# A fused transformer layer: a new start for the first batch (x ahead of five weights, rope from PSUM, smaller pieces, 20 maxima ahead of the first key-major product)

## The chip, the cores and the metric

One core of one Trainium2 chip. The metric is device time in microseconds (us) of one launch; the median of three runs before is 2280.6 us (2273.85 to 2281.94). The profile is one execution of the same program.

## The reference

The input x has 32 batches of 512 tokens by 256 channels, all in float32. Per batch:

```
x = x + attn(layernorm(x))      # q, k: x @ W.T with rope on pairs of channels, 16 heads of 16
                                # softmax(q k.T / 4) @ v, then @ Wu.T + bu
x = x + ffn(layernorm(x))       # xr, xk: token mixes of x and x shifted by one token
                                # sigmoid(xr @ Wr.T) * (relu(xk @ Wk.T)**2 @ Wv.T)
```

## The kernel before, in words

The work of every engine is written out by hand, in steps. Step b runs from -3 to 33, and each works on several batches at once: the attention of batch b, the projections of batch b+1 (v) and b+2 (q, k), the statistics of batch b+3 and the feed-forward part of batch b-1. Products in float32 are made of three products of high and low parts (`hi*hi`, `lo*hi`, `hi*lo`), so one q or k tile of 128 channels by 512 tokens has six matmuls in a PSUM bank, and a v tile has twelve of half the columns.

A step has 16 units (`UNITS`; a unit is one group of four heads by one quarter of the keys), and a unit has four places `j`. At each place TensorE makes one key-major product (`score_T`, line 893: keys in rows, scaled by the exponential on ScalarE, line 653) and one query-major product (`score`, line 911). VectorE takes the row maximum of the latter (line 694), 64 per batch. These maxima run ahead of the key-major products by `LEAD = 7` units: in step -1, units 9 to 15 make scores and maxima 0 to 27 of batch 0, and step 0 goes on with 28 to 63 and with the next batch's. The place of a maximum is given by `row_max_at`. When 16 maxima of a group of four heads are there, TensorE turns them (`row_max_T`, line 941, in unit 13 of the step ahead for group 0, and in units 1, 5 and 9 for groups 1 to 3, `MAX_T`), VectorE splits them into a high and a low part (`split_max`, lines 704 and 707), and four DMAs on SP's queue put them as two more rows under q (`move_max`, line 329). The key-major product of the group waits for these (`mrow_in`), so that the exponential comes out with the maximum subtracted. After the places, the unit's `values` (line 925) sums the probabilities of the unit before times v.

Next to the second place of every unit, TensorE has some dense work (`DENSE`): v in units 1 and 2, the turn of x in unit 3 (line 949), q in 6 and 7, k in 9 and 10, products of the batches b-1 in the others. All of it shares the two banks of `d_ps`; `bank_reader` says which reader must be done before a bank is written again. The second k product uses the bank of the first one.

ScalarE copies q and k out of PSUM into `rope_t` (line 577), which has room for one tensor; GpSimd (POOL) makes the rope in six operations (lines 411 to 429) in `rot`, ScalarE makes the high part (line 583), and GpSimd the low part (line 435). For batch 0 VectorE does the rope (`first_rope`, lines 808 to 817) and the low part (`first_low`, line 824). SP stores the parts to `scratch` (`store_parts`, line 356, t is 0 for q and 1 for k) and loads them back as stacks of three copies of 16 rows (`load_stacks`, line 305), in two halves of four slots: `stack_in` counts the first, `stack2_in` the second. Between the two stands the load of x for batch b+3 (`load_x`, line 347).

Ahead of the steps TensorE turns seven weights (line 877) into `d_ps`, `st_ps` and `s_ps`, and VectorE splits them (`turned_weight`, lines 679 and 683). All seven are turned ahead of step -2; VectorE splits four ahead of step -2 and three ahead of step -1. In an engine's queue everything runs in the order written; `extras` on ScalarE and VectorE says behind which place of which unit a piece stands. GpSimd's order has the scales of the statistics (`scales`, line 473) of batch b+3 ahead of the low part of batch b+2's q and the rope of its k.

Of the kernel before, what the change touches and what calls it, by code (L numbers as in the profile page):

```python
# [35 lines left out]
GH = 4  # L36
# [3 lines left out]
LEAD = 7  # L40
COPIES = 3
# [38 lines left out]
def layer_kernel(nc, x, wq, wk, wv, wu, bu, w_r, w_k, w_v, mu_r, mu_k, cos_t, sin_t, out):  # L80
    scratch = nc.dram_tensor("parts_scratch", [2, 2, 2 * D, H * T], F32)
    with ExitStack() as ctx:
# [91 lines left out]

        dve_passed, sp_passed = sem("dve_passed"), sem("sp_passed")
# [73 lines left out]
        def _(sp):  # L249
            sp.dma_start(xn[:, :, :], x[0].rearrange("(c p) d -> p c d", p=P)).then_inc(x_in, 16)  # L250
            for w, src in enumerate((wq, wk, wv, wu, w_r, w_k, w_v)):
                dst, src = probs[:, w // GH, w % GH, :], src.rearrange("(o p) c -> p o c", p=P)
                if WEIGHTS[w] != "u":
                    sp.dma_start(dst.rearrange("p (o c) -> p o c", o=CB), src).then_inc(w_qk_in if w < 2 else w_in, 16)
                    continue
                for e in range(2):
                    for o in range(CB):
                        sp.dma_start(dst.rearrange("p (o i e c) -> p o i e c", o=CB, i=CB, e=2)[:, :, o, e, :],
                                     src.rearrange("p o (e i c) -> p o e i c", e=2, i=CB)[:, :, e, o, :]).then_inc(w_in, 16)
            sp.dma_start(cos_sb[:, :], cos_t).then_inc(c_in, 16)  # L260
            sp.dma_start(sin_sb[:, :], sin_t).then_inc(c_in, 16)
            sp.dma_start(bu_sb[:, :], bu.rearrange("(a c) -> a c", a=1).to_broadcast([P, C])).then_inc(c_in, 16)
            for n, mu in enumerate((mu_r, mu_k)):
                for o in range(CB):
                    sp.dma_start(mu_sb[:, n, o:o + 1],
                                 mu[o * P:(o + 1) * P].rearrange("(p a) -> p a", a=1)).then_inc(c_in, 16)

# [6 lines left out]
            def step(b, par):  # L274
# [9 lines left out]
                def load_stacks(go):  # L284
# [11 lines left out]
                    n, slots = 1 - par, slice(go * PAIRS // 2, (go + 1) * PAIRS // 2)  # L296
                    for half in range(2):
                        row, at = 64 * half, (2 * half + go) * PAIRS // 2 * T
                        src_q, src_k = [scratch[n, t][:, at:at + PAIRS // 2 * T] for t in range(2)]
                        twice = bass.AP(src_q.tensor, src_q.offset, [[H * T, D], [0, 2], [1, PAIRS // 2 * T]])  # L300
                        both = bass.AP(src_k.tensor, src_k.offset, [[H * T, D], [D * H * T, 2], [1, PAIRS // 2 * T]])
                        for dst, at, count, src in ((q_st[n], row, 2 * D, twice), (k_st[n], row, 2 * D, both),
                                                    (q_st[n], row + 2 * D, D, src_q[D:2 * D]),
                                                    (k_st[n], row + 2 * D, D, src_k[0:D])):
                            sp.dma_start(dst[at:at + count, slots, :].bitcast(F32).rearrange("p h t -> p (h t)"),
                                         src).then_inc((stack_in, stack2_in)[go], 16)
# [42 lines left out]
                def store_parts(s, half, t):  # L349
                    if s.active():  # L350
# [708 lines left out]
```

## Time and profile before

| | us |
|---|---|
| median of 3 runs (lowest, highest) | 2280.6 (2273.85, 2281.94) |
| time of the profiled execution | 2281.66 |
| its span, first to last instruction | 2279.9 |
| TensorE matmuls busy | 2124.2 (93%) |
| VectorE busy | 2067.4 (91%) |
| ScalarE busy | 1645.7 (72%) |
| GpSimd busy | 1391.3 (61%) |
| mean granted TensorE clock | 0.979 |

The span is what the profile covers; the time of the execution has 1.8 us more around it. Busy times of TensorE are modelled ends of pipelined matmuls. The steps of the middle of the run take 67 to 68 us each. A number in a row is the start in us from the span's beginning, the one behind it the duration; in brackets stands the idle time ahead of it and what ended it.

### The profile page before, as it was taken

The numbers are of one execution on the slowest core, as the hardware profiler recorded it, in microseconds if no ns is written. First come the engines' busy times: TensorE is split into PE (matmuls) and PEld (weight loads), VectorE is DVE, ScalarE is ACT, GpSimd is POOL, SyncE is SP. The second block draws the span as 40 slices with busy tenths as digits, with TensorE's granted clock in tenths as the row PEclk, the third lists the DMA queues.
The fourth block names the chain that finished last, engine by engine and source line by source line (L and its number), as shares of the span: only waits on it lengthen the run. The fifth ranks groups of instructions, "written<-read, shape, count | busy, mean of one in ns | idle before, by whom it ended". The sixth has DMA issues, their size and how long they took to land.

```text
span 2279.9 us, 39602 instructions
## 1 busy us (share of the span) xinstructions
PE 2124.2 (93%) x13084; PEld 1093.3 (48%) x13084; DVE 2067.4 (91%) x3982; ACT 1645.7 (72%) x3137; POOL 1391.3 (61%) x1184
## 2 busy tenths in 40 slices
PE   4999999999999999999999999999999999999995
PEld 3445444445454455444445444444545444545443
DVE  5899999999999999999999999999999999999862
ACT  2477777777777777777777777777777777777662
POOL 5347766666766666776566676566676566576334
PEclk8799999999999999999999999999999999999987
DMA  6544445544355554444564444554435555444410
GB/s 150 110 107 103 104 91 130 129 111 103 95 106 113 129 128 101 103 98 98 128 131 106 102 100 91 129 129 115 98 96 106 113 129 123 102 103 93 89 29 24
DMA packets 133466, 242.09 MB, mean 106 GB/s; under 512 B 24848, under 2 KB 79760, under 8 KB 120976
## 3 DMA queue, kind: packets, MB, share of 16 engines
q1 hardware_dynamic: 133264, 239.56, 46.7%
q8 instruction: 106, 1.74, 0.3%
q14 instruction: 96, 0.79, 0.1%
HBM read 136.71 MB, written 83.89 MB: 97 GB/s over the span
## 4 chain that ended last, share of the span: by engine, by line
PE 42%; DVE 32%; issue 10%; SPq 4%; POOL 4%; ACT 4%; DMA 3%; DVEq 0%; POOLq 0%; ACTq 0%
PE d_ps L955 17%; DVE mx L694 17%; PE st_ps L893 12%; PE pv_ps L925 8%; POOL f_lo L465 4%; PE s_ps L911 3%; DVE sums L718 3%; SPq L318 2%; DVE ve L759 2%; PE d_ps L949 2%; SPq L329 2%; ACT probs L653 2%; DVE stats L748 2%; DVE attn L730 2%; DMA q_st<-mparts 1%
## 5 line engine op out<-in xcount | busy, mean ns | idle before, releaser
L653 ACT ACTIVATE probs<-st_ps 128x512 f32<-128x512 f32 x2048 | 1154.8, 597 | 505.2 <-PE st_ps L893 483.6
L694 DVE TENSOR_REDUCE mx<-s_ps 128x1 f32<-128x512 f32 x2048 | 1324.4, 676 | 117.4 <-PE s_ps L911 114.1
L893 PE MATMUL st_ps<-q_st,k_st 50*128 50x512 f32 x2048 | 804.4, 459 | 45.7 <-ACT probs L653 29.8
L911 PE MATMUL s_ps<-k_st,q_st 48*128 48x512 f32 x2048 | 815.8, 464 | 30.8 <-DVE mx L694 20.8
L893 PEld LDWEIGHTS st_ps<-q_st,k_st 50*128 50x128 f32 x2048 | 324.1, 186 | 664.3 <-ACT probs L653 450.5
L925 PE MATMUL pv_ps<-probs,v_ext 128*32 128x512 f32 x4096 | 549.7, 609 | 0.2 <-DVE sums L718 0.2
L473 POOL TENSOR_TENSOR rs<-ve,mhalf 128x2 f32<-128x2 f32 x128 | 90.3, 706 | 444.7 <-DVE mean L760 444.7
L911 PEld LDWEIGHTS s_ps<-k_st,q_st 48*128 48x128 f32 x2048 | 327.2, 186 | 61.7 <-DVE mx L694 50.8
L465 POOL TENSOR_TENSOR f_lo<-yn,f_hi 128x512 fp32r<-128x512 f32 x128 | 175.2, 1379 | 107.8 <-ACT f_hi L618 107.8
L435 POOL TENSOR_TENSOR parts<-parts 128x1024 fp32r<-128x1024 f32 x62 | 148.1, 2389 | 60.4 <-ACT parts L583 60.4
L723 DVE TENSOR_TENSOR sums<-sums,inv 128x256 f32<-128x256 f32 x128 | 164.0, 1281 | 4.4
L925 PEld LDWEIGHTS pv_ps<-probs,v_ext 128*32 128x32 f32 x4096 | 81.1, 108 | 179.1 <-issue 176.9
L451 POOL TENSOR_TENSOR r_lo<-xrT,r_hi 128x512 fp32r<-128x512 f32 x64 | 82.4, 1287 | 101.9 <-ACT r_hi L598 101.9
L458 POOL TENSOR_TENSOR f_lo<-attnT,f_hi 128x512 fp32r<-128x512 f32 x64 | 82.5, 1289 | 71.2 <-ACT f_hi L606 71.2
L618 ACT ACTIVATE f_hi<-yn 128x512 fp32r<-128x512 f32 x128 | 80.9, 632 | 27.8 <-DVE yn L791 22.5
L718 DVE STREAM_TRANSPOSE sums<-pv_ps 128x512 f32<-128x512 f32 x128 | 89.4, 698 | 11.3 <-PE pv_ps L925 11.3
L577 ACT ACTIVATE rope_t<-d_ps 128x512 f32<-128x512 f32 x128 | 76.7, 599 | 29.1 <-PE d_ps L955 26.3
L394 POOL TENSOR_TENSOR gate<-gate,y 128x512 f32<-128x512 f32 x64 | 87.0, 1359 | 16.9 <-DVE gate L800 16.9
L411 POOL TENSOR_TENSOR parts<-rope_t,sin_sb 128x512 f32<-128x512 f32 x62 | 79.6, 1284 | 28.2 <-ACT rope_t L577 28.2
L417 POOL TENSOR_TENSOR rope_t<-rope_t,cos_sb 128x512 f32<-128x512 f32 x62 | 79.2, 1277 | 19.4 <-ACT rope_t L577 14.1
L420 POOL TENSOR_TENSOR rope_t<-rope_t,sin_sb 128x512 f32<-128x512 f32 x62 | 86.5, 1395 | 4.8
L730 DVE STREAM_TRANSPOSE attn<-sums 128x512 f32<-128x512 f32 x128 | 89.2, 697 | 0.1
(116 smaller groups left out, 3959.4 us busy)
## 6 DMA issues: line engine op xcount, KB each, us to landing
parts_scratch<-parts SPq DMA_DIRECT2D x64, 1024.0 KB, 4.5
q_st<-parts_scratch SPq DMA_DIRECT2D x128, 256.0 KB, 5.5
k_st<-parts_scratch SPq DMA_DIRECT2D x128, 256.0 KB, 6.6
xn<-in_L_attn_x_dram SPq DMA_DIRECT2D x32, 512.0 KB, 9.2
q_st<-parts_scratch SPq DMA_DIRECT2D x128, 128.0 KB, 7.0
k_st<-parts_scratch SPq DMA_DIRECT2D x128, 128.0 KB, 7.4
attnT<-attn SPq DMA_DIRECT2D x512, 32.0 KB, 2.0
y<-in_L_attn_x_dram SPq DMA_DIRECT2D x32, 512.0 KB, 6.5
```

The lines of the kernel that those rows point to most:

```text
L435: nc.gpsimd.tensor_tensor(parts[:, t, 1, :, :], rot[:, t, :, :], parts[:, t, 0, :, :], ALU.subtract).then_inc(sub2, 1)
L465: nc.gpsimd.tensor_tensor(f_lo[:, o, :], mixT[:, o, :], f_hi[:, o, :], ALU.subtract).then_inc(f_lo_done, 1)
L473: nc.gpsimd.tensor_tensor(rs[:, a:z], ve[:, a:z], mhalf[:, :], ALU.pow).then_inc(scale, 1)
L653: nc.scalar.activation(probs[:, u % SLOTS, j, :], st_ps[:, n % 2, :], ACT.Exp, scale=float(D) ** -0.5).then_inc(exp_done, 1)
L694: nc.vector.tensor_reduce(mx[:, col:col + 1], s_ps[:, ring_bank(n), :], AX.X, ALU.max).then_inc(max_done, 1)
L718: nc.vector.transpose(sums[:, :], pv_ps[:, 0, :]).then_inc(norm_step, 1)
L723: nc.vector.tensor_tensor(blocks[:, :, 0:D], blocks[:, :, 0:D], inv[:, :].rearrange("p (k r) -> p k r", r=1) .to_broadcast([P, T // 32, D] ...
L730: nc.vector.transpose(attn[:, :], sums[:, :]).then_inc(attn_done, 1)
L893: nc.tensor.matmul(st_ps[:, n % 2, :], k_st[par][row:row + SROWS + MROWS, slot, c * P:(c + 1) * P], q_st[par][row:row + SROWS + MROWS, slo ...
L911: nc.tensor.matmul(s_ps[:, ring_bank(n), :], q_st[at][row:row + SROWS, slot, qc * P:(qc + 1) * P], k_st[at][row:row + SROWS, slot, :], sta ...
L925: ins = nc.tensor.matmul(pv_ps[32 * j:32 * j + 32, 0, :], v_ext[half][:, c, VW * h:VW * h + 32], probs[:, u % SLOTS, j, :], start=(c == 0) ...
L955: ins = nc.tensor.matmul(bank, w[a], x[z], start=first and k == 0, stop=last and k == 2)
```

## The change

All of it concerns the first batches; the steps from 1 on are as before.

- SP loads the tables ahead of the last five weights. TensorE turns the first two weights, runs steps -3 and -2, and then turns the other five; VectorE splits v's weight ahead of step -1 and the other four inside unit 4 of step -1.
- In batch 0 the rope reads q and k straight from PSUM; ScalarE's copy of it goes.
- In batch 0 the high part and the low part of each tensor are stored by separate DMAs (`first_out` counts the high ones), and the first half of the stacks is loaded as two quarters (`first_in` counts the first of them), with the x of batch 2 between them.
- `BEGIN = 5`: step -1 makes 20 maxima of batch 0 in units 11 to 15, not 28 in units 9 to 15, thus behind both k products of batch 1. In step 0 two more scores and maxima stand behind each of the units 0, 2, 4 and 6.
- The turn of maxima of group 0 of batch 0 moves from unit 13 to 15, its split to places 2 and 3 of unit 15; group 1's moves from unit 1 to 2.
- The statistics of batches 1 and 2 are put together, those of batch 1 behind both low parts of batch 0, those of batch 2 behind the split in unit 15 of step -1.
- In step 0 SP moves the maxima of group 1 ahead of the store of batch 1's k parts.

```diff
@@ helpers
+BEGIN = 5
         def row_max_at(b, u, j):
+            if first(b.plus(1)):
+                n = GH * (u - UNITS + BEGIN) + j
+                return (b.plus(1), n) if n >= 0 else (b, SCORES - 1)
             n = GH * (u + LEAD) + j
+            if first(b) and u < GH * (LEAD - BEGIN):
+                n -= GH * (LEAD - BEGIN) - 2 * ((u + 1) // 2)
             return (b, n) if n < SCORES else (b.plus(1), n - SCORES)
+        def more_maxima(b, u):
+            if first(b) and u % 2 == 0 and u < GH * (LEAD - BEGIN):
+                return [row_max_at(b, u, GH + k) for k in range(2)]
+            return []
@@ sync, load_stacks and store_parts
-                    n, slots = 1 - par, slice(go * PAIRS // 2, (go + 1) * PAIRS // 2)
+                    if first(s) and go == 0:
+                        sp.wait_ge(first_out, 32)
+                        stack_slots(0, PAIRS // 4, first_in)
+                        load_x()
+                        stack_slots(PAIRS // 4, PAIRS // 4, stack_in)
+                    else:
+                        stack_slots(go * PAIRS // 2, PAIRS // 2, (stack_in, stack2_in)[go])
...
-                    if s.active():
+                    if first(s):
+                        for k, (made, stored) in enumerate(((hi_done, first_out), (sub2, parts_out))):
+                            sp.wait_ge(made, (2 * t + 2, t + 1)[k])
+                            sp.dma_start(scratch[half, t].rearrange("(k r i) (h c) -> k (i h) r c", k=2, r=2, h=H)[k],
+                                         parts[:, t, k, :, :].bitcast(F32)).then_inc(stored, 16)
+                    elif s.active():
...
+                if first(b):
+                    move_max(b, 1)
                 store_parts(b.plus(1), 1 - par, 1)
                 move_attn(b.plus(-1), 3)
-                move_max(b, 1)
+                if not first(b):
+                    move_max(b, 1)
                 store_out()
                 load_stacks(0)
-                load_x()
+                if not first(b.plus(1)):
+                    load_x()
@@ scalar
                 def qk_evac(t, r):
                     s = b.plus(2)
-                    if s.active():
+                    if s.active() and not first(s):
@@ vector, first_rope
-                    dve.wait_ge(qk_done, 2 * t + 1)
-                    nc.vector.tensor_tensor(rot[:, t, 1, :], rope_t[:, 0, :], sin_sb[:, :], ALU.mult).then_inc(rope_step, 1)
-                    nc.vector.tensor_tensor(rot[:, t, 0, :], rope_t[:, 0, :], cos_sb[:, :], ALU.mult).then_inc(rope_step, 1)
+                    even, odd = [d_ps[:, BANK["QK"[t], r], :] for r in range(2)]
+                    dve.wait_ge(qk_ready, 2 * t + 1)
+                    nc.vector.tensor_tensor(rot[:, t, 1, :], even, sin_sb[:, :], ALU.mult).then_inc(rope_step, 1)
+                    nc.vector.tensor_tensor(rot[:, t, 0, :], even, cos_sb[:, :], ALU.mult).then_inc(qk_done, 1)
...
@@ vector, extras
+                stats = [(stats1_of, 0, 0), (stats1_of, 0, 1), (stats1_of, 1, 0), (stats1_of, 1, 1)]
+                if first(b.plus(2)) or first(b.plus(1)):
+                    for at in [at for at, work in extras.items() if work[0] in stats]:
+                        extras.pop(at)
                 if first(b.plus(2)):
-                    extras[5, 0] = [(normalise, b, 0, 0), (first_rope, 0), (first_rope, 1), (first_low, 0)]
-                    extras[7, 3] = extras.pop((8, 3)) + extras.pop((9, 1)) + extras.pop((14, 1)) + extras.pop((14, 3))
-                    extras[8, 0] = [(first_low, 1)]
+                    extras[5, 0] = [(first_rope, 0), (first_rope, 1), (first_low, 0), (first_low, 1)] + stats
+                if first(b.plus(1)):
+                    extras[4, 1] = [(turned_weight, w, WEIGHTS[w]) for w in range(3, 7)]
+                    extras[15, 2], extras[15, 3] = extras.pop((13, 2)), extras.pop((13, 3)) + stats
+                if first(b):
+                    extras[2, 2], extras[2, 3] = extras[1, 3][1:], extras.pop((2, 0))
+                    extras[1, 3] = extras[1, 3][:1]
@@ tensor
-                    if n == 0:
+                    if first(s) and n == 0:
+                        pe.wait_ge(first_in, 128)
+                        pe.wait_ge(wT_done, 7)
+                    if n == (SCORES // 4 if first(s) else 0):
                         pe.wait_ge(stack_in, s.count(128, 128))
...
+                    for s, n in more_maxima(b, u):
+                        score(s, n)
...
             for b in range(FIRST, -1):
                 step(Seq(b), b % 2)
-            pe.wait_ge(wT_done, 4)
+            pe.wait_ge(w_in, 16 * 8)
+            for w in range(2, 7):
+                turn_weight(w)
+            pe.wait_ge(wT_done, 3)
             pe.wait_ge(const_ok, 8)
             steps(pe, step, -1)
```

## Rows read from the trace of the kernel before

**Rows 1.** Chain of waits, 0 to 150 us: start us, us, what

```profile
18.20 3.01 PE d_ps L955 x12
...
25.31 2.05 PE d_ps L955 x6
...
35.63 4.26 DMA parts_scratch<-parts
...
44.68 12.47 DMA xn<-in_L_attn_x_dram
...
60.72 2.86 PE d_ps L955 x6
```

**Rows 2.** Timeline, 0 to 41 us: start us, us, engine line op out<-in xcount

```profile
10.54 1.14 DVE L683 SCALAR_TENSOR_TENSOR w_lo_k<-d_ps,w_hi_k 128x64 fp32r<-128x64 f32 x8
...
14.96 1.62 PE L949 MATMUL d_ps<-ident,xn 128*128 128x128 f32 x8
...
16.77 1.29 DVE L780 TENSOR_TENSOR xnT_lo<-d_ps,xnT_hi 128x512 fp32r<-128x512 f32 x2 [1.47 <-ACT xnT_hi L544]
...
20.49 0.69 DVE L808 TENSOR_TENSOR parts<-rope_t,sin_sb 128x512 f32<-128x512 f32 x1 [2.44 <-ACT rope_t L577]
...
30.62 1.21 DVE L824 TENSOR_TENSOR parts<-parts 128x1024 fp32r<-128x1024 f32 x1
...
34.38 1.22 DVE L824 TENSOR_TENSOR parts<-parts 128x1024 fp32r<-128x1024 f32 x1
...
35.96 0.58 PE L955 MATMUL d_ps<-w_hi_v,xnT_hi 128*128 128x256 f32 x1 [4.84 <-ACT v_ext L534]
...
39.84 0.88 DVE L683 SCALAR_TENSOR_TENSOR w_lo_fv<-s_ps,w_hi_fv 128x128 fp32r<-128x128 f32 x4
```

**Rows 3.** Timeline, 42 to 78 us

```profile
42.06 0.48 PE L955 MATMUL d_ps<-xnT_hi,w_hi_q 128*128 128x512 f32 x1 [1.63 <-DVE xnT_lo L780]
...
44.41 1.28 POOL L411 TENSOR_TENSOR parts<-rope_t,sin_sb 128x512 f32<-128x512 f32 x1 [7.99 <-ACT rope_t L577]
...
50.83 1.26 POOL L429 TENSOR_TENSOR parts<-parts,rope_t 128x512 f32<-128x512 f32 x1
...
53.74 0.80 PE L911 MATMUL s_ps<-k_st,q_st 48*128 48x512 f32 x2 [8.66 <-DMA k_st<-parts_scratch]
...
64.22 8.08 DVE L694 TENSOR_REDUCE mx<-s_ps 128x1 f32<-128x512 f32 x13 [2.29 <-PE s_ps L911]
...
73.01 0.27 DVE L707 SCALAR_TENSOR_TENSOR mparts<-d_ps,mparts 16x128 fp32r<-16x128 f32 x1
...
77.56 0.33 PEld L893 LDWEIGHTS st_ps<-q_st,k_st 50*128 50x128 f32 x1
```

**Rows 4.** Timeline of step 0, 83 to 110 us

```profile
83.79 2.37 POOL L435 TENSOR_TENSOR parts<-parts 128x1024 fp32r<-128x1024 f32 x1 [5.98 <-ACT parts L583]
...
88.22 0.50 PE L893 MATMUL st_ps<-q_st,k_st 50*128 50x512 f32 x1
...
89.70 2.69 SPq L329 DMA_DIRECT2D q_st<-mparts  x4
...
95.48 0.49 PE L893 MATMUL st_ps<-q_st,k_st 50*128 50x512 f32 x1
...
98.87 0.50 PE L893 MATMUL st_ps<-q_st,k_st 50*128 50x512 f32 x1
...
99.55 0.28 PE L941 MATMUL d_ps<-ident,mx 128*16 128x128 f32 x1
...
109.81 0.50 PE L893 MATMUL st_ps<-q_st,k_st 50*128 50x512 f32 x1
```

**Rows 5.** Windows: us, busy time of PE, PEld, DVE, ACT, POOL, granted clock, DMA share, GB/s

```profile
36.00:38.00 2.00, 2.00 (x9) 2.00 (x10) 1.97 (x10) 1.09 (x2) 0.35 (x2) 0.50 0.75 284
```

**Rows 6.** Chain of the whole span: first and last of 30 low parts, once a step

```profile
182.23 2.92 POOL f_lo L465 x2
...
2142.59 2.90 POOL f_lo L465 x2
```

More of the change, by code:

```diff
@@ L266, in _ @@
                                  mu[o * P:(o + 1) * P].rearrange("(p a) -> p a", a=1)).then_inc(c_in, 16)
+            for w, src in enumerate((wv, wu, w_r, w_k, w_v)):
+                load_weight(w + 2, src)
             def carry_wait(b):
@@ new lines, in stack_slots @@
+                def stack_slots(lo, count, landed):
+                    n, slots = 1 - par, slice(lo, lo + count)
+                    for half in range(2):
+                        row, at = 64 * half, (half * PAIRS + lo) * T
+                        src_q, src_k = [scratch[n, t][:, at:at + count * T] for t in range(2)]
+                        twice = bass.AP(src_q.tensor, src_q.offset, [[H * T, D], [0, 2], [1, count * T]])
+                        both = bass.AP(src_k.tensor, src_k.offset, [[H * T, D], [D * H * T, 2], [1, count * T]])
+                        for dst, at, rows, src in ((q_st[n], row, 2 * D, twice), (k_st[n], row, 2 * D, both),
+                                                   (q_st[n], row + 2 * D, D, src_q[D:2 * D]),
+                                                   (k_st[n], row + 2 * D, D, src_k[0:D])):
+                            sp.dma_start(dst[at:at + rows, slots, :].bitcast(F32).rearrange("p h t -> p (h t)"),
+                                         src).then_inc(landed, 16)
@@ L870, in _, with turn_weight @@
             pe.wait_ge(w_qk_in, 16 * 2)
-            for w in range(7):
-                if w == 2:
-                    pe.wait_ge(w_in, 16 * 8)
+            def turn_weight(w):
                 src = probs[:, w // GH, w % GH, :].rearrange("p (o c) -> p o c", o=CB)
@@ L1008, in dense @@
                         token_rows(b.plus(-2) if name == "O1" else prev, "O", int(name[-1]), half, weight("fv"), (f_hi, f_lo), f_lo_done, 4, 4, o_ready)
+                max_T = dict(MAX_T)
+                if first(b):
+                    max_T[2] = max_T.pop(1)
+                if first(b.plus(1)):
+                    max_T[15] = max_T.pop(13)
                 for u in range(UNITS):
@@ L1012, in step @@
                         score_T(u, j)
-                        score(u, j)
+                        score(*row_max_at(b, u, j))
                         if j == 1:
@@ L1016, in step @@
                             dense(u, 1)
-                            if u in MAX_T:
-                                d, g = MAX_T[u]
+                            if u in max_T:
+                                d, g = max_T[u]
                                 row_max_T(b.plus(d), g)
+                    for s, n in more_maxima(b, u):
+                        score(s, n)
                     if u == 0:
```

50 lines of the change are left out of this document (23 added, 27 removed).

## Prediction, made before the change was run

> **What bounds the kernel now.** I read the chain of waits over the first 150 us, then the timeline from 0 to 145 us engine by engine, since everything that the diff touches runs before the second batch. The chain is a single thread up to 40 us: products of q and k [rows 1], VectorE's rope and low parts, then the store of the parts until 39.9 us. The first score product then stands 8.66 us for its stacks, until 53.74 [rows 3]; meanwhile VectorE waits for an x load that took 12.47 us behind the stack loads [rows 1], in front of its maxima. 28 maxima and two more products of six follow, and the first key-major product (ST below) starts at 77.56 [rows 3]. From there a unit (four ST, four scores, dense work, eight value products) takes 3.3 to 4 us: 21.31 us up to unit 5 and 32.25 up to unit 8 [rows 4]. So the change can act in two stretches: before ST, 77.56 us, and in units 0 to 7 of batch 0.
>
> **Part 1: x and rope before the weights.** The turn of x starts behind all seven weights at 14.96; after it starts when w_lo_k is done, 10.54 + 1.14 = 11.68, say 11.75 [rows 2]. The 3.24 us from there to the first q product (18.20) stay: it starts at 15.0. Six matmuls are half of 3.01 [rows 1]; with the signal, q's even half is ready at 16.65. The copies on ScalarE go. VectorE: two operations, at 0.62 each as the maxima of the same width follow one another [rows 3], to 17.9; odd half at 18.0; four more to 20.5; k's even two to 21.75; the second k product, 2.05 [rows 1], to 23.85; four operations to 26.3; low parts 2 x 1.15 to 28.6. Before, the second ended at 34.38 + 1.22 = 35.6 [rows 2]. Gain 7.0. 4.4 of it is in the ropes; 2.6 is the statistics that stood between the two low parts and now come behind them. If the clock is low at q already, its six matmuls take 2.86 [rows 1], so each of two products costs 1.3 more: 26.3 becomes at worst 29.
>
> A multiply with a PSUM operand is bounded by the subtraction of xnT, which reads PSUM: 1.29 for two, against 0.69 for one from SBUF [rows 2]. I take no difference. The Trainium skill's page "VectorE: DVE Perf Modes", section on the TRN2 errata, gives an access of PSUM 62 cycles more than one of SBUF, 0.065 us at its 0.96 GHz; by it eight multiplies would be 0.5 us later. The rows here do not show it.
>
> **Part 2: parts and stacks in pieces.** The high parts of q leave at about 21; at 27.5 to 28.8 three pieces of half a tensor follow, 1.5 MB. One whole part alone took 4.26 [rows 1]; half as many bytes more, so 4.3 to 6.4; the last landed at 33.3. Before it was 39.9. Stacks: 24 issues in place of 16, at most 0.67 each by the moves of maxima [rows 4], 5.4 us of SP's queue. The first eight end at 38.5; with their own landing they are there by 44 to 48. Behind them SP stands for the turn of x of batch 1 (40 us, below), then x and the other pieces; even with 12.47 us each is there long before score 32. All of this is covered, because the wait for the stacks is not last any more:
>
> **Part 3: what comes before the first score.** PE turns five weights after the last k product (20 transposes at 0.2 by [rows 2], to 28) and waits for the weights of v. VectorE: low parts to 28.6, four statistics 34.38 - 30.62 - 1.13 = 2.6 to 31.2, weights of v two groups of four at 0.88 [rows 2] to 33.0. v's first product starts at 33.1, with the low clock seen at 36 to 38 us (0.50, that is 1.2 GHz) [rows 5]. Its 12 matmuls and the copy are some 3.6, so the second starts at 36.7; from there to q of batch 1 it was 42.06 - 35.96 = 6.1 [rows 2, 3]; q starts at 42.8. VectorE turns the last four weights in 4 x 1.76 = 7 to 49.7: covered. q ready and copied (44.41 - 42.06 = 2.35) at 45.15; POOL's six rope operations 50.83 + 1.26 - 44.41 = 7.7 [rows 3] to 52.85. Now comes what decides: k's two products of batch 1 stand ahead of the first score in PE's order (BEGIN is 5, LEAD was 7); the first copy of k needs rope_t free, the second k product needs that copy. So it starts at 53.55, where before the scores had begun; then 3.5 us from 60.72 to the maximum at 64.22 [rows 1, 3]. First maximum at 57.1.
>
> Twenty maxima at 8.08/13 = 0.62 [rows 3], with the two halves of the split 12.9, so the split ends at 70.0. From the end of the split to ST it was 77.56 - 73.28 = 4.28 [rows 3]: ST at 74.2, 3.4 earlier. Bounds for this sum: every product of v, x and k at the high clock (1.5 for 2.86, and nearly as much for 12 of half the columns) takes some 4.5 off; stacks that land 13 us after their issue add nothing, as they are still there before 55; q's low clock adds 2.7.
>
> **Part 4: units 0 to 7 take on the other eight.** Each even unit has two more scores and maxima. PE pays 8 x 0.25 = 2 us at least, some more at the low clock. More where a transpose of maxima stands in order. (a) Group 1 moves from unit 1 to 2, and its split's second half behind the sixth maximum of unit 2. Before, the split's rows went out at 89.70, 1.48 after unit 2's start, and unit 4 started at 95.48 without waiting [rows 4]. Now unit 2 is 1.1 longer (group transpose, two scores, a wait for VectorE) and the split ends 6 us after its start, just inside unit 3; with 4.28, unit 4's ST opens 10.3 us after unit 2's start instead of 95.48 - 88.22 = 7.26: +3.0, of which 0.3 comes back in unit 1. (b) Unit 4: six maxima and a subtraction, 6 x 0.61 + 0.65 = 4.3, against a unit of 3.39 (95.48 to 98.87): +0.9. (c) Unit 5: group 2 needs 48 maxima. Before, the 49th and 50th scores were out, its transpose ran 0.68 into the unit [rows 4]; now number 48 is the score just issued, and VectorE has the two of unit 4, one, a transposition of sums and this one ahead: the transpose runs 2.4 into it: +1.75. (d) Two more scores in units 0 and 6: +0.4 (low clock) and +0.5. (e) POOL: batch 2's statistics now stand behind the split, at 70 to 72.6, and POOL's scales stand ahead of low part 1 (2.37) [rows 4] and the six ropes of k (7.7): the sum that ScalarE wants at unit 0 is there at 81.2, where before it was ready ahead of ST. ScalarE stands from 77.6 to 81.2; the first v product of batch 1 (12 matmuls at the low clock) covers all but about 0.5. Sum 2.7 + 0.9 + 1.75 + 0.9 + 0.5, some +6.7.
>
> SP in step 0: the store of batch 1's k parts moves behind the move of maxima, from 83.79 + 2.37 = 86.2 [rows 4] to about 94. Its stacks then land by about 112, and unit 9 wants them at about 117, x at 113 for 116.6. Hidden; without that cover up to 3 us.
>
> The Trainium skill's page "DMA: Bandwidth & Descriptors", section "Rules for kernel authors", says to coalesce many small transfers and gives a megabyte or more per DMA for full bandwidth, so it speaks against the pieces. By it the loads would be slower; by the row, x of 512 KB stood 12.47 us in the queue, and even so the pieces would be in time.
>
> **Sum.** -3.4 + 6.7 = +3.3 us. The profiled execution's own time is 2281.66 (span 2279.9, 1.8 around it); so 2285. It is 1.1 above the median of the three runs, 2280.6 (2273.85 to 2281.94); against that: 2284, called no change, for 0.5% is 11.4 us, about what a measurement of this kernel can tell.
>
> **Rivals.** (A) The forecast, a gain handed back by the gates of part 4: 2280 to 2288. Chance 0.5. (B) The gain is kept: the gates cost only the two scores and the POOL wait (2.5), as VectorE has slack in these units; 2281.7 - 3.4 + 2.5 = 2281, and with the clock high in step -1 another 4.5 to 2276. For it: VectorE is idle between the split and ST. Against: a, b and c are orders, not averages. Chance 0.32, 2272 to 2281. (C) Slower: the late store of batch 1's parts decides. If its stacks take as long as x in step -1 (12.47), they land at 104 + 12.5 = 116.5, and x, next in the queue, near 117, beyond 116.6; each us beyond it stops VectorE in unit 8 ahead of the last maxima of its batch. With the bounds of part 2 this is +3 to +8 on the forecast: 2288 to 2292; beyond 2292 only with q's low clock too. Chance 0.11. (D) The 29 steps between [rows 6] have 67.6 us on the mean, (2142.59 - 182.23)/29; another phase of the queues may move all by 0.4: 12 us to either side. Chance 0.07. That the change does not do what it says would be an x that is not normalised by 11.7; the statistics of batch 0 are done by then in the weights' shade, so this has no chance of its own.
>
> **Range and chances.** 2274 to 2292 holds A, most of B and C. Faster by over 0.5% (under 2269) needs D or all of B's bounds: 0.05. Slower by over 0.5% (over 2292) needs C at its end or D: 0.07. Within: 0.88.
>
> **What would show it.** Low parts' second operation ending near 28.6; first score not before 55, released by ScalarE's copy of k and not by a stack DMA; ST near 74; ScalarE standing for POOL at unit 0; PE standing for the moved maxima at unit 4 (about 2 us) and for a maximum at unit 5; unit 8 starting near 113, against 109.81. ST before 71, or unit 8 before 109, makes A wrong and B right; VectorE standing for x or PE for stacks in units 8 and 9 is C; a mean step off 67.6 by 0.3 is D.

## The result, and the profile after

The changed kernel takes 2290.4 us in the median of 6 runs (2288.16 to 2297.18), the kernel before 2281.27 (2273.85 to 2284.43, 6 runs). The ratio is 1.0051, with a 95% interval of 1.0035 to 1.0066. It is slower by 9.1 us between the medians, where 3.3 were forecast; by the interval of the ratio it is 8.0 to 15.1 us. The number lies inside the forecast's range, but the forecast's "no change" and its 2284 are wrong, and it lies in the band of rival C (2288 to 2292), whose cause is not what happened. The profiled execution took 2290.01 us, span 2288.2, against 2281.66 and 2279.9 before.

The busy line of the page after shows nothing of it; the difference is in waits and in a clock, in the first 120 us:

```profile
PE 2124.4 (93%) x13084; PEld 1094.3 (48%) x13084; DVE 2073.2 (91%) x3982; ACT 1644.1 (72%) x3133; POOL 1389.5 (61%) x1184
```

The chain of waits after (start us, us, what) has a new opening, and then the low clock of step 0. In that step two waits have appeared, which are called gates below: places of TensorE's fixed order where it must stand until something has arrived.

```profile
15.14 5.47 PE d_ps L1007 x12
...
29.63 2.27 DVE parts L864 x2
...
36.71 2.94 PE d_ps L1007 x12
...
57.35 2.92 PE d_ps L1007 x6
...
61.05 0.69 DVE mx L732
...
77.75 0.80 PE st_ps L945
...
102.04 1.86 PE pv_ps L977 x8
```

The twelve products of q (even and odd half) took 5.47 us, where they took 3.01 before [rows 1]. No DMA stands ahead of the scores any more. Yet ST, the first key-major product, starts at 77.75, where it started at 77.56 [rows 3]. ST and the starts of units are given by the weight load that opens them.

TensorE's timeline after, from ST to unit 8 (start us, us, line, operation, count, [idle before <- what ended it]):

```profile
77.75 0.79 PE L945 MATMUL st_ps<-q_st,k_st 50*128 50x512 f32 x1 [5.62 <-DMA q_st<-mparts]
...
87.93 0.50 PE L945 MATMUL st_ps<-q_st,k_st 50*128 50x512 f32 x1
...
98.14 0.50 PE L945 MATMUL st_ps<-q_st,k_st 50*128 50x512 f32 x1 [1.58 <-DMA q_st<-mparts]
...
101.97 1.93 PE L977 MATMUL pv_ps<-probs,v_ext 128*32 128x512 f32 x8
...
103.84 0.79 PE L945 MATMUL st_ps<-q_st,k_st 50*128 50x512 f32 x1
...
106.64 0.38 PE L993 MATMUL d_ps<-ident,mx 128*16 128x128 f32 x1 [1.59 <-DVE mx L732]
...
118.90 0.50 PE L945 MATMUL st_ps<-q_st,k_st 50*128 50x512 f32 x1
```

These are units 0, 2, 4, 5 and 8. Unit 2 still starts where it did (87.93, before 88.22 [rows 4]). Unit 4 stands 1.58 us for the moved maxima, and the transpose of group 2 in unit 5 stands 1.59 us for a maximum. Between the two the eight value products take 1.93 us; before they took 1.06 at this place. TensorE's timeline and a window of the kernel before:

```profile
97.88 1.06 PE L925 MATMUL pv_ps<-probs,v_ext 128*32 128x512 f32 x8
```

```profile
100.00:102.00 2.00, 1.94 (x14) 0.56 (x14) 2.00 (x5) 1.59 (x4) 0.00 (x0) 1.00 1.25 197
```

The windows after (us, busy time of PE, PEld, DVE, ACT, POOL, granted clock, DMA share, GB/s) show what differs:

```profile
98.00:100.00 2.00, 1.41 (x8) 0.67 (x8) 1.29 (x3) 1.23 (x3) 0.00 (x0) 0.93 1.02 381
100.00:102.00 2.00, 1.96 (x8) 0.70 (x9) 2.00 (x4) 1.05 (x2) 0.00 (x0) 0.50 0.12 44
...
108.00:110.00 2.00, 2.00 (x12) 0.23 (x10) 1.29 (x3) 0.87 (x2) 0.00 (x0) 0.51 1.06 197
110.00:112.00 2.00, 2.00 (x14) 1.31 (x10) 1.46 (x3) 1.09 (x2) 0.00 (x0) 1.00 0.93 98
```

The granted clock falls from 1.00 to 0.50, 2.4 to 1.2 GHz, near 99.8 us, behind the first of the two waits, and comes back at about 110. Before it was 1.00 in every window from 98 to 108.

From ST to unit 8 it is 41.15 us (118.90 - 77.75), against 32.25 before: +8.9, and with ST's 0.2 unit 8 starts 9.1 us later. That this is also the difference of the medians is in part chance: a second profile of the kernel before, among the experiments, has unit 8 at 107.33, 11.6 us ahead of the changed kernel's. Its units 0 and 1 took 9.49 us, in the first profile 10.66, where the eight value products of unit 1 took 1.59 us and not 1.07. Behind unit 8 the kernels are alike: from the first low part f_lo of the whole chain (190.87; before 182.23 [rows 6]) to the end of the span it is 2097.3 us after and 2097.7 before.

### The profile page after: what moved, and what is told of

Its sections match the earlier page's. It is cut to its first block, busy times and chain, and to the rows that moved or that the text cites. A ratio compares the mean times of both kernels' runs of the same rounds, so it can differ in the third digit from the quotient of the medians.

```text
span 2288.2 us, 39610 instructions
## 1 busy us (share of the span) xinstructions
PE 2124.4 (93%) x13084; PEld 1094.3 (48%) x13084; DVE 2073.2 (91%) x3982; ACT 1644.1 (72%) x3133; POOL 1389.5 (61%) x1184
## 3 DMA queue, kind: packets, MB, share of 16 engines
q8 instruction: 106, 1.74, 0.3%
## 4 chain that ended last, share of the span: by engine, by line
PE 42%; DVE 31%; issue 10%; POOL 5%; SPq 5%; ACT 4%; DMA 3%; DVEq 0%; POOLq 0%; ACTq 0%
PE d_ps L1007 18%; DVE mx L732 16%; PE st_ps L945 11%; PE pv_ps L977 8%; POOL f_lo L504 4%; PE s_ps L963 4%; DVE sums L756 3%; SPq L346 3%; SPq L357 2%; DVE ve L797 2%; DMA q_st<-mparts 2%; PE d_ps L1001 2%; DVE attn L768 2%; ACT probs L692 2%; DVE y L778 1%
## 5 line engine op out<-in xcount | busy, mean ns | idle before, releaser
L622 ACT ACTIVATE parts<-parts 128x512 fp32r<-128x512 f32 x128 | 80.5, 630 | 16.8 <-DVE parts L855 13.6
```

## Experiments

Each kernel has 6 to 12 runs, and runs of the kernel before beside them, whose medians were 2279.11 to 2281.94; so the ratios compare, and the medians of two rows less well. "Unit 8" is the start of its first key-major product; "rest" is the span less the start of the first f_lo. The rest differs by up to 10.6 us from profile to profile. ST scatters too: "after", "gate of unit 5 eased", "all eight early" and the latter with the old store order are one and the same order of work up to ST, and have 77.75, 75.93, 75.73 and 77.70, according to how soon the clock rose during q (its twelve products took 5.47, 4.85, 4.54 and 5.47 us). So mechanisms are read from single waits and from ST to unit 8, and the sum from the ratio. Two of the recorded expectations give the distance from ST to unit 8 of an earlier kernel as 38.9 and 34.9; by the traces it is 38.10 and 34.14.

| kernel | ST | unit 8 | ST to unit 8 | rest | median | ratio [95%] |
|---|---|---|---|---|---|---|
| before | 77.56 | 109.81 | 32.25 | 2097.7 | | |
| before, again | 76.24 | 107.33 | 31.09 | 2098.4 | 2280.69 | 0.9997 [0.9981, 1.0014] |
| after | 77.75 | 118.90 | 41.15 | 2097.3 | 2290.4 | 1.0051 [1.0035, 1.0066] |
| 20 maxima alone | 75.80 | 117.64 | 41.84 | 2091.8 | 2291.33 | 1.0043 [1.0027, 1.0059] |
| 28 maxima, rest of the change | 74.54 | 108.68 | 34.14 | 2100.6 | 2284.27 | 1.0020 [1.0007, 1.0034] |
| the same, old store order | 74.45 | 106.55 | 32.10 | 2099.0 | 2284.62 | 1.0010 [0.9991, 1.0029] |
| the same, with fillers | 73.03 | 105.36 | 32.33 | 2096.6 | 2278.28 | 0.9990 [0.9975, 1.0005] |
| gate of unit 5 eased | 75.93 | 114.47 | 38.54 | 2100.9 | 2291.23 | 1.0043 [1.0029, 1.0057] |
| all eight maxima early | 75.73 | 113.83 | 38.10 | 2101.2 | 2289.89 | 1.0040 [1.0024, 1.0055] |
| the same, old store order | 77.70 | 112.36 | 34.66 | 2099.0 | 2287.6 | 1.0020 [1.0006, 1.0035] |
| one filler | 77.30 | 119.74 | 42.44 | 2101.5 | 2292.28 | 1.0053 [1.0036, 1.0070] |
| two fillers | 74.92 | 117.48 | 42.56 | 2102.4 | 2292.34 | 1.0037 [1.0022, 1.0053] |
| seven weights first | 78.25 | 120.68 | 42.43 | 2101.7 | 2295.13 | 1.0053 [1.0034, 1.0073] |
| all the repairs, 20 maxima | 74.55 | 109.30 | 34.75 | 2095.7 | 2280.11 | 0.9998 [0.9984, 1.0012] |

**One filler: the clock of q.** Twelve transposes of the identity, which nobody reads, fill TensorE's wait for x.

```diff
             turn_weight(1)
+            for k in range(12):
+                nc.tensor.transpose(st_ps[:, 0, (k % 4) * P:(k % 4 + 1) * P], ident[:, :], ident[:, :])
             pe.wait_ge(wT_done, 2)
```

> The changed kernel, with 12 more transposes of the identity into a free bank of st_ps between the turn of the first two weights and the turn of x, where TensorE stood idle; nothing else. Theory 1 (clock): the new start took from TensorE the 20 transposes that stood just ahead of q's products, so it comes to them at the low level: 12 q matmuls took 5.47 us, 3.01 before. With the filler they take 3.0 to 3.3, VectorE's second low part ends near 29.3 and not 31.9, the first key-major product (ST) comes at about 75 and not 77.75, and the span falls by 2 to 3 us against the changed kernel. Theory 2 (the slow q products have another reason, such as the DMAs beside them): q stays at 5.4, ST stays at 77.7. Neither expects anything of units 0 to 7 of step 0: still some 41 us from ST to unit 8.

The turn of x ran at the upper level, but behind the next 1.74 us of idle time q had lost it. TensorE's timeline of this kernel:

```profile
11.75 1.09 PE L1003 MATMUL d_ps<-ident,xn 128*128 128x128 f32 x8 [1.04 <-DVE w_lo_k L722]
...
14.58 0.76 PE L1009 MATMUL d_ps<-xnT_hi,w_hi_q 128*128 128x512 f32 x1 [1.74 <-DVE xnT_lo L818]
15.14 0.63 PE L1009 MATMUL d_ps<-xnT_lo,w_hi_q 128*128 128x512 f32 x1
```

and of the changed kernel:

```profile
11.67 1.97 PE L1001 MATMUL d_ps<-ident,xn 128*128 128x128 f32 x8 [3.27 <-DVE w_lo_k L722]
...
15.14 0.76 PE L1007 MATMUL d_ps<-xnT_hi,w_hi_q 128*128 128x512 f32 x1 [1.50 <-DVE xnT_lo L818]
15.70 0.63 PE L1007 MATMUL d_ps<-xnT_lo,w_hi_q 128*128 128x512 f32 x1
```

q's twelve took 5.47 us again, low parts ended at 31.5, ST came at 77.30: the expected gain was missed, which left open whether the clock was the cause at all.

**Two fillers.** Another twelve in the gap between the turn of x and q:

```diff
                         if j == 1:
+                            if first(b.plus(2)) and u == 5:
+                                for k in range(12):
+                                    nc.tensor.transpose(st_ps[:, 0, (k % 4) * P:(k % 4 + 1) * P], ident[:, :], ident[:, :])
                             dense(u, 0)
```

> The changed kernel with two fillers on TensorE: 12 transposes of the identity while VectorE splits the first two weights, and 12 more between the turn of x and q's products, both into a free bank. With the first alone the turn of x ran at the upper level (1.09 us for 8, 1.97 without) and q again at the lower one after an idle 1.7 us. Clock theory: without the idle gap q's 12 products take 3.0 to 3.3 us in place of 5.5, ST comes 2 to 3 us before the changed kernel's 77.75. Rival (transposes do not hold the level, whatever is put there): q at 5.4, ST at 77 or later.

```profile
12.75 1.47 PE L1076 MATMUL st_ps<-ident 128*128 128x128 f32 x12
...
14.66 0.47 PE L1009 MATMUL d_ps<-xnT_hi,w_hi_q 128*128 128x512 f32 x1 [0.43 <-DVE xnT_lo L818]
14.97 0.40 PE L1009 MATMUL d_ps<-xnT_lo,w_hi_q 128*128 128x512 f32 x1
```

Now q's 12 products take 3.02 us in place of 5.47, low parts end at 29.1 and ST is at 74.92, 2.8 earlier. The clock of q was what Part 1 lacked. It is q's twelve products that carry this, and not ST, whose scatter is 2 us: they took 3.02 in all three kernels with both fillers, and 4.54 to 5.47 in the seven profiles of the new start with one filler or none (the one with seven weights first is apart). The total did not move (ratio 1.0037, overlapping the change's): ST to unit 8 took 42.56.

**The gate of unit 5.** The late maxima follow units 0, 2, 3 and 4 in place of 0, 2, 4 and 6:

```diff
-                n -= GH * (LEAD - BEGIN) - 2 * ((u + 1) // 2)
+                n -= GH * (LEAD - BEGIN) - 2 * (0, 1, 1, 2, 3, 4, 4, 4)[u]
...
-            if first(b) and u % 2 == 0 and u < GH * (LEAD - BEGIN):
+            if first(b) and u in (0, 2, 3, 4):
```

> The changed kernel with the eight late scores and maxima behind units 0, 2, 3 and 4 in place of 0, 2, 4 and 6; their number stays. Group 2's transpose in unit 5 then has number 50 issued and needs 48. Theory 1 (order): the wait of 1.6 us ahead of that transpose goes; the one of 1.6 us at unit 4 for the moved maxima of group 1 stays; ST to unit 8 falls from 41.2 to between 37.5 and 39.5, the less if the clock still falls at 100 us. Theory 2 (load: the eight maxima themselves fill VectorE and TensorE): it stays within 0.7 of 41.2.

Up to unit 8 the number of scores and maxima is that of the changed kernel; only their order differs. TensorE's timeline and a window:

```profile
96.34 0.50 PE L945 MATMUL st_ps<-q_st,k_st 50*128 50x512 f32 x1 [0.52 <-DMA q_st<-mparts]
...
99.88 1.06 PE L977 MATMUL pv_ps<-probs,v_ext 128*32 128x512 f32 x8
...
101.55 0.28 PE L993 MATMUL d_ps<-ident,mx 128*16 128x128 f32 x1
```

```profile
100.00:102.00 2.00, 1.82 (x13) 0.42 (x10) 1.74 (x3) 0.59 (x2) 0.00 (x0) 1.00 0.76 197
```

The wait in unit 5 is gone, the one in unit 4 is 0.52, the clock stays at 1.00 in these units and the value products are back at 1.06 us. Units 4 and 5 take 4.54 and 3.09 us (5.69 and 6.14 in the changed kernel), and unit 6, rid of its two late scores, 1.1 less. But unit 8 now waited for the moved maxima of group 2: its weight load stood 3.50 us, of which 0.84 is there in the kernel before too, and the matmuls 2.59. So only 2.6 of 5.3 us arrived there. The ratio, 1.0043, cannot be told from the change's. Behind this wait the clock fell: unit 8's value products took 1.94 us.

**All eight early.** Two behind each of units 0 to 3, and behind VectorE's other work of the unit:

```diff
-                n -= GH * (LEAD - BEGIN) - 2 * ((u + 1) // 2)
+                n -= GH * (LEAD - BEGIN) - 2 * min(u, LEAD - BEGIN + 2)
...
-            if first(b) and u % 2 == 0 and u < GH * (LEAD - BEGIN):
+            if first(b) and u < LEAD - BEGIN + 2:
...
-                        if qc == TC - 1:
-                            for s, n in more_maxima(b, u):
-                                row_max(s, n)
...
+                    for s, n in more_maxima(b, u):
+                        row_max(s, n)
```

> The changed kernel with the eight late scores and maxima behind units 0, 1, 2 and 3, and on VectorE behind that unit's other work, so that the second half of the split of group 1 stands ahead of two of them. Number of everything unchanged. Theory 1 (order and clock): unit 4 waits at most 0.7 us for the moved maxima, unit 5 does not wait, the granted clock stays at its upper level from 88 us on, and ST to unit 8 falls from 41.2 to 35 to 37 (32.25 before). Theory 2 (load): it stays above 39. Span against the changed kernel: theory 1 4 to 6 us less, theory 2 within 2.

Both gates of units 4 and 5 went and the clock stayed up to unit 8, but ST to unit 8 took 38.10 us where 35 to 37 were expected. SyncE's queue of this kernel, the weight load that opens unit 8, and the value products of that unit:

```profile
103.52 0.42 SPq L375 DMA_DIRECT2D xn<-in_L_attn_x_dram  x1
104.19 2.78 SPq L357 DMA_DIRECT2D q_st<-mparts  x4
```

```profile
113.83 0.18 PEld L944 LDWEIGHTS st_ps<-q_st,k_st 50*128 50x128 f32 x1 [4.28 <-DMA q_st<-mparts]
...
116.46 1.93 PE L976 MATMUL pv_ps<-probs,v_ext 128*32 128x512 f32 x8
```

The rows of group 2 were issued at 104.19, right behind eight stack loads and x of 0.5 MB, and were there only at 113.83: 9.6 us. The matmuls stood 3.37 us for them, and behind that the clock fell here too.

**All eight early, with the old store order.** The store of batch 1's k parts, and so the stacks and x behind it, goes ahead of the move of group 1 again.

```diff
-                if first(b):
-                    move_max(b, 1)
                 store_parts(b.plus(1), 1 - par, 1)
...
-                if not first(b):
-                    move_max(b, 1)
+                move_max(b, 1)
```

> The kernel with the eight late maxima behind units 0 to 3, and in addition SP stores batch 1's k parts ahead of the move of the maxima of group 1, as before the change. Without the latter, unit 8 stood 4.3 us for the maxima of group 2: their four DMAs were issued at 104.19, just behind the stack and x loads, and took until 113.83. Theory 6 (the late store pushes those loads against the maxima's move): now the store goes at about 88, the loads at 92 to 98, unit 8 waits less than 1 us, and ST to unit 8 is 35 to 36.5 (38.9 without). Rival (the maxima's move is slow for another reason): unit 8 still waits 3 to 4 us.

```profile
100.82 0.42 SPq L375 DMA_DIRECT2D xn<-in_L_attn_x_dram  x1
106.14 2.76 SPq L357 DMA_DIRECT2D q_st<-mparts  x4
```

```profile
112.36 0.18 PEld L941 LDWEIGHTS st_ps<-q_st,k_st 50*128 50x128 f32 x1 [0.84 <-issue]
```

The loads were issued 2.7 us earlier, though ST was 2 us later. The rows of group 2 were issued 5.3 us behind x, and unit 8 no longer waited for them; the 0.84 us left is there in the kernel before too. ST to unit 8 fell from 38.10 to 34.66, below the 35 to 36.5 expected, so the late store costs 3.4 us as soon as the gates before it are gone (2.0 with 28 maxima, below). In the changed kernel it was covered: there group 2's rows were issued at 111.44 only, 5.85 behind x's.

**28 maxima, all else new.** BEGIN is 7 again, the statistics of batch 2 and the transposes and splits of groups 0 and 1 are at their old places. The late store stays.

```diff
-BEGIN = 5
+BEGIN = 7
...
-                    extras[2, 2], extras[2, 3] = extras[1, 3][1:], extras.pop((2, 0))
...
-                    max_T[2] = max_T.pop(1)
```

> The changed kernel with 28 maxima ahead again, in units 9 to 15 of step -1, and the maxima's transposes, splits and the statistics of batch 2 at their old places; the new start, the rope from PSUM and the small pieces stay. Theory 1: step 0 takes its old 32.3 us from ST to unit 8; the first six maxima are made while GpSimd still works on q of batch 1, the rest behind the second k product (60 us), so ST comes at 74.5 to 76 and the span is 2 to 4 us below the kernel before, 10 to 12 below the changed one. Theory 3 (the early part alone is at fault: the pieces and the queue make it slow): ST comes at 78 or later and the span is no better than before.

ST came at 74.54, earlier than with 20 (75.73 with low parts from 27.80 us; here they start at 27.90), although eight more maxima are asked for. VectorE's timeline of this kernel and then of the changed one shows where those eight are:

```profile
52.44 1.29 DVE L732 TENSOR_REDUCE mx<-s_ps 128x1 f32<-128x512 f32 x2 [0.28 <-PE s_ps L959]
...
56.05 2.48 DVE L732 TENSOR_REDUCE mx<-s_ps 128x1 f32<-128x512 f32 x4 [1.09 <-PE s_ps L959]
...
61.20 8.08 DVE L732 TENSOR_REDUCE mx<-s_ps 128x1 f32<-128x512 f32 x13 [2.67 <-PE s_ps L959]
69.19 0.27 DVE L742 TENSOR_SCALAR mparts<-d_ps 16x128 fp32r<-16x128 f32 x1
```

```profile
61.04 11.67 DVE L732 TENSOR_REDUCE mx<-s_ps 128x1 f32<-128x512 f32 x19 [7.77 <-PE s_ps L963]
72.62 0.27 DVE L742 TENSOR_SCALAR mparts<-d_ps 16x128 fp32r<-16x128 f32 x1
```

2 + 4 + 13 = 19 maxima stand ahead of the split that ST waits for, and 19 in the changed kernel too. The others ran behind the split, while its rows were under way (4.28 us before, [rows 3]). Taking eight away from there takes nothing off the path. And six of the 19 were done in the shade of k's products of batch 1, which now stand ahead of all. Then unit 8 waited for the rows of group 2:

```profile
108.68 0.18 PEld L941 LDWEIGHTS st_ps<-q_st,k_st 50*128 50x128 f32 x1 [3.08 <-DMA q_st<-mparts]
```

The matmuls of unit 8 stood 2.17 us for them. The ratio, 1.0020, is above 1, where a span 2 to 4 us below before was expected: the start's gain had been turned into that wait.

**28 maxima and the old store order.** Both edits together.

> The kernel with 28 maxima ahead again, and with SP's order of step 0 as before the change. Without the latter unit 8 stood 3.1 us for the maxima of group 2. Theory 6: that wait goes, ST to unit 8 falls from 34.9 to 32.3, unit 8 starts 3 us ahead of before, and the median lies 0 to 5 us below before. Rival: the wait stays, and the median is that of the kernel without this edit, 3 to 4 us above before.

```profile
106.55 0.18 PEld L938 LDWEIGHTS st_ps<-q_st,k_st 50*128 50x128 f32 x1 [0.84 <-issue]
```

The wait is gone, and ST to unit 8 is 32.10. But the expected 0 to 5 us below before did not come, the ratio being 1.0010 [0.9991, 1.0029]: the start alone is worth 1.8 us at ST against the control (3.1 against the first profile) and nothing that the median shows.

**28 maxima, the old store order and both fillers**, the best of these kernels:

> The version that the runs so far point to: the changed kernel's new start, rope from PSUM and small pieces, with 28 maxima ahead, SP's old order in step 0, and both fillers (12 transposes of the identity ahead of the turn of x and 12 behind it). Each edit's effect as seen alone: q's 12 products 3.0 us, second low part ending near 29, ST 1.5 to 2.8 us before the 74.45 of the version without fillers, unit 8 near 104 (109.8 and 107.2 in the two traces of before). Median 3 to 6 us below before. Against it: the gain ahead of ST is lost in the waits for GpSimd's rope, then it equals the version without fillers, 0 to 3 us above before.

ST is at 73.03 (71.65 to 72.95 expected) and unit 8 at 105.36 (near 104 expected), where the two profiles of the kernel before have 109.81 and 107.33. The median is 0.8 us below that of before, where 3 to 6 were expected, ratio 0.9990 [0.9975, 1.0005]: better than the changed kernel beyond doubt, not to be told from the one before.

**The kernel before, again**, as a control:

> The kernel before, unchanged, as a control with a trace of its own. Theory 4 (what follows step 0 differs by chance from one execution to the next): its first f_lo pair starts near 182.2 again, and the 28 steps from there may take 1893 us (as in the first trace of before) or 1896 to 1898 (as in the changed kernels). Theory 5 (the changed start leaves the steady steps longer): they take 1893 us within 1.5, and the changed kernels' 3 to 4 us more there are theirs.

The 28 steps behind the first f_lo took 1898.7 us (180.68 to 2079.40), in the first profile 1892.8 (182.23 to 2075.05), in the changed kernel 1897.0 (190.87 to 2087.88). Executions of one kernel differ there by more than the change does.

**20 maxima alone**, on the kernel before: the counts, the order of the extras and the transposes of the diff; x, rope, parts and stores as before.

```diff
+BEGIN = 5
...
+            if first(b) and u < GH * (LEAD - BEGIN):
+                n -= GH * (LEAD - BEGIN) - 2 * ((u + 1) // 2)
...
+                    extras[2, 2], extras[2, 3] = extras[1, 3][1:], extras.pop((2, 0))
+                    extras[1, 3] = extras[1, 3][:1]
...
+                    max_T[2] = max_T.pop(1)
```

> The kernel before with one part of the change alone: 20 maxima ahead, the eight others behind units 0, 2, 4 and 6, group 0's transpose in unit 15 and group 1's in unit 2; start, rope, pieces, statistics and SP's order as before. Theory 1: ST comes at 75.5 to 77.5 (76.2 and 77.6 before), and ST to unit 8 grows by 6 to 9 us from 32.3, with waits at units 4 and 5 and perhaps the clock falling behind them; the median is 6 to 9 us above before. If most of the changed kernel's loss comes from its start, it is within 3 us of before.

TensorE's timeline of this kernel:

```profile
95.22 0.49 PE L912 MATMUL st_ps<-q_st,k_st 50*128 50x512 f32 x1 [1.08 <-DMA q_st<-mparts]
...
103.71 0.38 PE L959 MATMUL d_ps<-ident,mx 128*16 128x128 f32 x1 [1.59 <-DVE mx L705]
```

```profile
98.00:100.00 2.00, 2.00 (x10) 0.49 (x10) 2.00 (x4) 0.07 (x1) 0.00 (x0) 0.50 1.23 148
...
108.00:110.00 2.00, 2.00 (x6) 1.49 (x5) 1.37 (x3) 0.95 (x2) 0.00 (x0) 0.50 0.00 0
```

The waits are at the same two places, the clock falls as it did, ST to unit 8 is 41.84 us, 9.6 more than in the first profile of before (6 to 9 were expected), and the ratio of 1.0043 overlaps the change's. This part alone loses as much as the whole change, within the intervals; its ST is 0.4 us ahead of the control's.

**Seven weights first**, in the changed kernel:

```diff
             turn_weight(1)
+            pe.wait_ge(w_in, 16 * 8)
+            for w in range(2, 7):
+                turn_weight(w)
             pe.wait_ge(wT_done, 2)
```

> The changed kernel with all seven weights turned ahead of x again; nothing else. The turn of x goes back from 11.7 to near 15.0 us, but TensorE has worked right up to it. Clock theory: q's products take 3.0 to 3.3 us, not 5.5, so that the second low part ends at 31.5 to 33 (31.9 with x first) and ST at 77.3 to 79 (77.75): x ahead of the weights has gained nothing. Without the clock effect it would be 3.3 us later: ST at 81.

```profile
17.34 1.36 PE L1004 MATMUL d_ps<-ident,xn 128*128 128x128 f32 x8
...
20.44 0.47 PE L1010 MATMUL d_ps<-xnT_hi,w_hi_q 128*128 128x512 f32 x1 [1.74 <-DVE xnT_lo L818]
```

q ran at the upper level, the low parts ended at 34.1 and ST came at 78.25. x was turned 5.7 us later, and not near 15.0 as expected: SP's new order brings the tables ahead of the last five weights, so these came later than before, and this kernel does not give the old start back. ST is within its bounds and 0.5 us behind the changed kernel's, less than ST's scatter. In the new load order x ahead of five weights puts q 5.3 us earlier (15.14 for 20.44) and gives 2.4 of them back in q's clock; against the kernel before q starts 3.1 us earlier (18.20) and ends 0.6 earlier.

**All the repairs with 20 maxima**: the early eight, the old store order, both fillers, and the statistics of batch 2 back ahead of the split.

> The changed kernel's 20 maxima kept, with all that the runs found mended around them: both fillers, the eight late ones behind units 0 to 3, SP's old order in step 0, and batch 2's statistics right behind the turned weights in step -1, so that ScalarE no longer stands for GpSimd in unit 0. ST near 75 as with the fillers alone, ST to unit 8 34 to 34.6 us (41.2 in the changed kernel, 32.3 before), so unit 8 near 109.3 and a median within 3 us of before. If order and clock are not all of it, unit 8 stays beyond 112.

Unit 8 at 109.30, ratio 0.9998 [0.9984, 1.0012]: the loss is taken back, nothing is won.

**All profiles together.** In step 0 the matmuls stood 1.08 to 1.62 us for moved maxima ahead of unit 4 in five kernels, and the value products behind that took 1.93 or 1.94 us. They stood 2.17 to 3.37 us ahead of unit 8 in three others, and those behind took 1.68 to 1.94. With a wait of 0.52 us ahead of unit 4, or with none, the value products at these places took 1.06 or 1.07.

## Why the prediction was wrong

**The step that failed** is the sum of Part 4, "some +6.7", on top of "ST at 74.2". What was wrong in both is one cost: the matmuls that follow a wait of TensorE were priced at the upper clock. The places of the waits were right, and so was the sign of Part 4. It came to 8.9, 2.2 more; ST came at 77.75, 3.5 late and so not earlier at all (ST's scatter of 2 us between equal kernels is part of this). With the forecast's 3.3 these make 9.0 of the 9.1 us. Shown by the runs:

- **Part 1**, low parts to 28.6: 31.9. "If the clock is low at q already, its six matmuls take 2.86" stood there as a bound; it was what happened, 5.47 for q's 12 and 2.74 for the six of k's second product (2.05 forecast). The two fillers gave 29.1. The forecast took the row of 3.01 for twelve at face, though in the changed order TensorE stands 3.27 us ahead of the turn of x and 1.50 ahead of q.
- **PSUM operand**: no difference, right. VectorE's timeline after has the multiply from PSUM at 0.68 us; the one from SBUF took 0.69 [rows 2]:

```profile
18.68 0.68 DVE L848 TENSOR_TENSOR parts<-d_ps,cos_sb 128x512 f32<-128x512 f32 x1
```

  The 62 cycles (0.065 us) of the Trainium skill's "VectorE: DVE Perf Modes", section on the TRN2 errata, do not show in this operation.
- **Parts 2 and 3**: all milestones kept their distances to within 0.7 us and came 3.5 to 4 us late, behind low parts that were 3.3 late: first product of v 36.71 (33.1), second k product 57.35 (53.55), first maximum 61.05 (57.1), ST 77.75 (74.2). No stack DMA released a score, as forecast. When q's clock is repaired, 2.8 us of ST's lateness go (against the earliest of the equal kernels 0.8).
- **Part 4, a to c**: waits of 1.58 us at unit 4 and 1.59 at unit 5 where about 2 and 1.75 were forecast. By units the growth was -0.5 for 0 and 1 together (+0.7 against the control), +1.21, +1.74, +2.3, +3.04, +1.09 for 2 to 6. Units 2 and 3 are as worked out, 2.95 for 3.0; units 4 and 5 were given 0.9 and 1.75 and cost 2.7 more: from 99.8 us on they ran at 1.2 GHz. The prediction priced the waits and the two extra scores, not what the waits do to the clock. With the gate of unit 5 eased, the clock stayed, and the two units took 2.6 us less beside the wait of 1.59 that went. Beside it, the Trainium skill's "TensorE: Matmul & The Clock Gate", section "HAM oscillation", tells of a kernel whose clock falls again and again behind DMA waits; the trace agrees in kind, with 0.50 granted behind the DMA wait of 1.58 us, once. A rival was missing that takes both low clocks together: the gain of 3.4 less the prediction's own 2.7 for q's low clock is 0.7; the gates' 6.7 and the 2.7 more that units 4 and 5 turned out to cost are 9.4; in sum +8.7. The second 2.7 was known only afterwards.
- **Part 4, e**: ScalarE stood 3.21 us for POOL (81.63 to 84.84), forecast 3.6 from 77.6 on and mostly hidden. Right in kind; its timeline after:

```profile
84.84 0.63 ACT L622 ACTIVATE parts<-parts 128x512 fp32r<-128x512 f32 x1 [3.21 <-POOL parts L465]
```

- **The late store** (rival C): hidden, as forecast, but only because the gates had delayed what it would have held up. "Without that cover up to 3 us" is about what three experiments show: the matmuls stood 2.17, 2.59 and 3.37 us, but for rows of 4 KB and not for the stacks. In the changed kernel nothing stood for x or the stacks in units 8 and 9, so that the median lies in C's band is not C's doing.
- **Rival B** fails with unit 8 at 118.90, and A's cause holds, but not its 2280 to 2288.
- **Rival D**: the steps behind are alike within what two executions of one kernel differ.

The loss, then: fewer maxima ahead of ST took nothing off the path, since 19 stand ahead of the split with 20 as with 28; x ahead of the weights started q 3.1 us earlier than before, but at half speed; and the eight moved maxima closed two gates whose waits also took the clock. "20 maxima alone" shows that the last suffices for a loss of this size (6.2 to 13.4 us by its interval). With all the repairs ST to unit 8 is still 34.75, 2.5 above the first profile of before and 3.7 above the control; by the prediction's 0.25 each, 2 of these are the eight scores themselves.

Not settled: what the best kernel's start is worth. Its unit 8 is 2.0 us ahead of the control's; its interval, -5.7 to +1.1 us, holds that and nothing at all. The rope from PSUM, the smaller pieces and the statistics put together were not run each by itself, so what each is worth is not shown.

## What to carry to other kernels

Work moved off the path to an in-order loop must be checked against every gate of that loop: what becomes due, which transfer carries it, what stands ahead of it in the issuing queue; and whether it was on the path at all is read by counting what stands ahead of the instruction that releases the next stage. Price a wait of TensorE with the matmuls behind it at the low clock as well (here 1.93 us for 1.06), and look at idle time ahead of a burst before taking its duration from another place. When a gate is opened, look for the next one at once: here it was a small transfer behind large ones.

## What the runs showed of the hardware

- At the start the granted clock of the windows does not always show the level that the matmuls run at. In the changed kernel it reads 1.00 from 16 to 18 us (below), and q's products start 0.43 us apart, as they do with one filler, where the same window reads 0.50; with two fillers they start 0.23 apart:

```profile
16.00:18.00 2.00, 2.00 (x6) 1.51 (x6) 0.00 (x0) 0.00 (x0) 1.89 (x3) 1.00 0.47 165
```

- A similar gap ahead of q had opposite outcomes: 1.74 us behind twelve fillers and eight turns left q at the low level, 1.74 us behind seven turned weights and eight turns left it at the upper, as in the control. So the length of the gap alone does not decide.
- The move of a group's maxima (four issues) took 9.6 us to arrive when it was issued 0.67 us behind x (512 KB) and eight stack loads in the same queue. Issued 1.73 and 1.92 us behind x it arrived after 8.9 and 8.5 us, and the matmuls of unit 8 stood 2.59 and 2.17 us for it; issued 5.3 us or more behind x it made none wait.
- In step 0 TensorE's clock fell behind single waits of 1.08 to 3.37 us in eight kernels, and not behind one of 0.52. Which length it takes, and what else plays a part, these runs do not show.
